# Causal top-8 attention in a ViT tower: keys from the centred stream, and a softmax shared out over DVE, ACT and Pool

## Chip, cores and metric

One core of a Trainium2 chip. The metric is the device time of one execution in microseconds (us). Engines: PE (TensorE, matmul), DVE (VectorE), ACT (ScalarE), Pool (GpSimd), SP (SyncE, which here only issues DMAs). All tiles of the passage are f32 unless said otherwise.

## The reference, cut to what matters

The kernel computes a tower of four layers on 16 images of 36 tokens with 64 features; after each attention and each feed-forward part stands `h = layernorm(h + part(h))`. The change lies in the attention of layer 2:

```python
Q = (x @ Wq.T).reshape(B, T, H, dh).transpose(0, 2, 1, 3)   # H = 4 heads, dh = 16, T = 36
K = (x @ Wk.T).reshape(B, T, H, dh).transpose(0, 2, 1, 3)
V = (x @ Wv.T).reshape(B, T, H, dh).transpose(0, 2, 1, 3)
scores = jnp.max(Q[:, :, :, None, :] + K[:, :, None, :, :], axis=-1)
scores = jnp.where(causal_mask[None, None], -jnp.inf, scores)
topk_vals, topk_idx = jax.lax.top_k(scores, k)              # k = 8
attn = jax.nn.softmax(topk_vals, axis=-1)
Vg = jnp.take_along_axis(V[:, :, None, :, :], topk_idx[..., None], axis=3)
ctx = jnp.einsum('bhtk,bhtkd->bhtd', attn, Vg)
```

The score is a maximum over a sum, not a dot product, and the softmax runs over the eight largest of the scores alone. `x` is the layer-normalised stream: centred per token, then multiplied by one over its standard deviation.

## The kernel before

576 tokens lie as [128, 288]: the two halves of the batch are stacked on partitions (64 features each), and a tile of 96 tokens per half is one of three (`NT` = 3, `TT` = 96). There are no loops over blocks of memory: each engine runs one long, hand-ordered list of instructions, and semaphores tie the lists together. An engine works its list strictly in order.

**Layernorm number k.** ACT squares the accumulated, already centred stream `psY` into `SQ` (semaphore `sq`). DVE copies it to `XC`, "centred" (`xc`). PE multiplies `SQ` with a mean matrix, which gives the variance with tokens on partitions (`variance(k)`, L376), ACT takes the root, DVE the reciprocal `RS`, [96 tokens, 6] (`rs`, L939). PE spreads `RS` over the features (`broadcast`, L383, called by `spread(k)`; `bc`), and DVE multiplies `XC` by it (`normalise(k, ...)`, L944), which gives `HP`, the normalised stream h (`hp`). `idle(n, bank)` (L369) issues n matmuls on a zero tile whose result nobody reads; they stand wherever PE would wait.

**Keys of layer 2.** For layernorm 4 PE runs `variance(4)`, `spread(4)`, waits for `hp`, and multiplies `HP` by `wk` (L589): the keys, with tokens on partitions, in PSUM (`k_done`). DVE splits them into three bf16 parts whose sum is the f32 value: `kp3[0]` a cast (L1149), the rest `k1f` a subtraction (L1151), `kp3[1]` a cast (L1152), `kp3[2]` a subtraction (L1154). Each adds one to `k_parts`. SP waits for each in turn and sends it to DRAM (L264); when all three have landed, one DMA brings them back, laid out by image, into `KB` (L267, `k_bcast`). Behind the keys PE makes queries (L592) and values (L598) out of `HP`; DVE, behind its key steps, splits the queries likewise (L1161 to L1168).

**Scores.** PE forms every sum q + k (L619, L621), and DVE takes the maximum over the 16 features of a head (L1177), 15 times, into `SC`, [128 queries, 5 x 4 rows, 40 keys], masked keys at -1e30.

**Softmax before.** On DVE: 20 `max` (MAX8, L1184) put the eight largest of each row, in order, into `top` (`topped`); 20 `match_replace` (L1188; each shows as a value load and a replacement) write to `REP` a copy of the row in which those eight are -3e30 (`replaced`). Then, each on all 20 x 40 elements of a partition: `REP` = (`SC` differs from `REP`), the selected ones (L1198); `SC` minus the row's maximum (L1199, `exp2_in`); ACT's exponential (L853, `exp2_out`); `PR` = the product with the selection (L1202); its row sum (L1203); reciprocal of 20 (L1204); `PR` times it (L1205, `prob2`). PE then transposes `PR` (L638), and the context follows. While it waits PE runs 7 dummy matmuls after the scores, 7 after `topped`, 7 after `replaced`, 4 after `exp2_in`, 7 after `exp2_out`.

Pool is in this time between two calls of `gates32` (L297), a small cast for the router, and has nothing to do.

## Time and profile before

| | us |
|---|---|
| median of 3 runs | 185.74 |
| lowest, highest | 184.01, 186.16 |
| the profiled execution: time | 185.84 |
| the profiled execution: span, first to last instruction | 184.1 |

| engine | busy us | share of the span |
|---|---|---|
| PE | 158.9 | 86% |
| DVE | 105.4 | 57% |
| ACT | 69.2 | 38% |
| Pool | 28.5 | 16% |

How to read it: a busy share is a mean over stages with different limits. PE's 86% holds 46.1 us of dummy matmuls, so it is no measure of a limit; what a stage is worth is read from the chain that ended last. In a row of a chain stand the start in us, the duration in us, and engine, tile and line. In a row of instruction groups stand the count, the busy time and the mean in ns of one, and behind the last bar the idle time before them.

### The profile page before, as it was taken

The numbers are of one execution on the slowest core, as the hardware profiler recorded it, in microseconds if no ns is written. First come the engines' busy times: TensorE is split into PE (matmuls) and PEld (weight loads), VectorE is DVE, ScalarE is ACT, GpSimd is POOL, SyncE is SP. The second block draws the span as 40 slices with busy tenths as digits, with TensorE's granted clock in tenths as the row PEclk, the third lists the DMA queues.
The fourth block names the chain that finished last, engine by engine and source line by source line (L and its number), as shares of the span: only waits on it lengthen the run. The fifth ranks groups of instructions, "written<-read, shape, count | busy, mean of one in ns | idle before, by whom it ended". The sixth has DMA issues, their size and how long they took to land.

```text
span 184.1 us, 2928 instructions
## 1 busy us (share of the span) xinstructions
PE 158.9 (86%) x1135; PEld 72.9 (40%) x1135; DVE 105.4 (57%) x324; ACT 69.2 (38%) x117; POOL 28.5 (16%) x79
## 2 busy tenths in 40 slices
PE   6999799899999988889978865699799997999950
PEld 2455366333333444334523121356333354573410
DVE  6224788454567374863756998716647422204884
ACT  3746906645460103634300000435723256563020
POOL 7300000187792000010000000000085000000000
PEclk9999999999999999999999999999999999996996
DMA  6999900000000000000220000000000000000001
GB/s 187 344 431 266 367 35 4 0 2 0 5 2 0 0 0 0 4 0 0 42 60 0 0 0 0 0 4 0 4 0 0 2 4 0 0 4 0 0 0 32
DMA packets 4916, 8.26 MB, mean 45 GB/s; under 512 B 2747, under 2 KB 2875, under 8 KB 4774
## 3 DMA queue, kind: packets, MB, share of 16 engines
q1 hardware_dynamic: 4902, 8.07, 13.5%
q8 instruction: 9, 0.15, 0.3%
q14 instruction: 5, 0.04, 0.1%
HBM read 7.70 MB, written 0.37 MB: 44 GB/s over the span
## 4 chain that ended last, share of the span: by engine, by line
PE 56%; DVE 27%; ACT 7%; DMA 5%; issue 3%; POOL 0%; DVEq 0%; ACTq 0%; POOLq 0%
PE ps L427 8%; PE ps L369 8%; PE ps L414 7%; DVE scores L1177 5%; PE ps L421 4%; PE ps L751 3%; PE ps L383 3%; PE ps L376 3%; DVE scores_rest L1188 2%; DMA k_scratch<-k_parts_tok 2%; DMA weights_sb<-weights 2%; PE ps L479 2%; PE ps L487 2%; DMA k_parts_img<-k_scratch 2%; DVE hidden_gated L998 2%
## 5 line engine op out<-in xcount | busy, mean ns | idle before, releaser
L369 PE MATMUL ps<-idle_operand 128*128 128x512 bf16 x170 | 46.1, 389 | 7.5 <-DVE scores_rest L1188 1.8
L998 DVE TENSOR_TENSOR hidden_gated<-hidden,ps 128x288 f32<-128x288 f32 x56 | 22.2, 450 | 14.6 <-PE ps L421 14.6
L787 ACT ACTIVATE hidden<-ps,weights_sb 128x576 f32<-128x576 f32 x28 | 20.2, 737 | 17.8 <-PE ps L414 15.4
L369 PEld LDWEIGHTS ps<-idle_operand 128*128 128x128 bf16 x170 | 14.5, 102 | 26.7 <-issue 5.3
L779 ACT ACT_TABLE_LOAD x16 | 20.5, 1283 | 0.3
L427 PE MATMUL ps<-hidden_gated,weights_sb 128*64 128x288 f32 x112 | 19.8, 432 | 0.9 <-DVE hidden_gated L998 0.8
L297 POOL CAST combine_parts_T<-combine_parts_T 48x288 f32<-48x288 bf16 x3 | 1.3, 418 | 105.6 <-DVE combine_parts_T L970 105.6
L767 ACT ACTIVATE squares<-ps 128x288 f32<-128x288 f32 x8 | 3.3, 410 | 33.6 <-PE ps L427 10.3
L414 PE MATMUL ps<-h,weights_sb 64*128 64x288 f32 x80 | 14.5, 449 | 1.0 <-ACT hidden L787 0.8
L936 DVE COPY centred<-ps 128x288 f32<-128x288 f32 x8 | 3.7, 456 | 18.0 <-ACT squares L767 18.0
L1177 DVE TENSOR_REDUCE scores<-ps 128x32 f32<-128x512 f32 (+1 forms) x15 | 8.8, 663 | 3.6 <-PE ps L621 3.6
L751 PE MATMUL ps<-weights_sb,hidden 128*128 128x512 f32 (+1 forms) x20 | 10.6, 689 | 0.0
L421 PE MATMUL ps<-combine_parts_T,selectors 128*128 128x288 bf16 x40 | 9.1, 292 | 0.8 <-DVE combine_parts_T L970 0.8
L414 PEld LDWEIGHTS ps<-h,weights_sb 64*128 64x128 f32 x80 | 6.3, 185 | 8.7 <-ACT hidden L787 4.7
L853 ACT ACTIVATE scores<-scores 128x800 f32<-128x800 f32 x1 | 0.9, 869 | 22.6 <-DVE scores L1199 22.6
L427 PEld LDWEIGHTS ps<-hidden_gated,weights_sb 128*64 128x64 f32 x112 | 5.5, 134 | 9.1 <-DVE hidden_gated L998 5.7
L414 PE MATMUL ps<-xn,weights_sb 64*128 64x288 f32 x32 | 5.6, 448 | 1.3 <-ACT hidden L787 1.3
L421 PEld LDWEIGHTS ps<-combine_parts_T,selectors 128*128 128x128 bf16 x40 | 3.0, 96 | 9.1 <-DVE hidden_gated L998 5.5
L751 PEld LDWEIGHTS ps<-weights_sb,hidden 128*128 128x128 f32 (+1 forms) x20 | 3.8, 199 | 6.3 <-issue 6.3
L376 PEld LDWEIGHTS ps<-consts_sb,squares 128*96 128x96 f32 x48 | 4.7, 164 | 3.9 <-ACT squares L767 3.9
L383 PE MATMUL ps<-consts_sb,rstd 96*64 96x96 f32 x108 | 6.2, 253 | 0.0
L619 PE MATMUL ps<-bconsts_sb,q_parts 128*128 128x512 bf16 (+1 forms) x15 | 5.7, 377 | 0.6 <-DMA k_parts_img<-k_scratch 0.6
(270 smaller groups left out, 225.4 us busy)
## 6 DMA issues: line engine op xcount, KB each, us to landing
patch_sb<-patches SPq DMA_DIRECT2D x6, 288.0 KB, 5.4
weights_sb<-weights SPq DMA_DIRECT2D x1, 1108.0 KB, 9.5
weights_sb<-weights SPq DMA_DIRECT2D x1, 717.0 KB, 15.5
weights_sb<-weights SPq DMA_DIRECT2D x1, 689.0 KB, 14.2
weights_sb<-weights SPq DMA_DIRECT2D x1, 640.0 KB, 7.3
weights_sb<-weights SPq DMA_DIRECT2D x1, 512.0 KB, 11.9
weights_sb<-weights SPq DMA_DIRECT2D x1, 394.0 KB, 12.9
weights_sb<-weights SPq DMA_DIRECT2D x1, 375.5 KB, 6.5
```

Of the source, the lines that this page charges most:

```text
L369: mm(PS[:, bank, :], idle_in[:, 0:P], idle_in[:, :], start=True, stop=True)
L376: last = mm(psVar[:, 2 * t:2 * t + 2], SQ[:, cols(t)], c("mean"), start=True, stop=True)
L383: last = mm(dst[rows(h), cols(t)], RS[:, at + 2 * t + h:at + 2 * t + h + 1].to_broadcast([TT, D]), c("ident", TT)[:, 0:TT], start=True, st ...
L414: last = mm(PS[:, z + h, 0:HALF], w1[rows(h), ch, :], src[rows(h), :], start=True, stop=True)
L421: mm(PS[:, G + h, 0:HALF], sel[:, g, h, :], CT3[:, :], start=True, stop=True)\
L427: last = mm(PS[rows(h), YB, 0:HALF], w2[:, ch, :], HG[:, ch % GRING, h, :], start=False, stop=(ch == chunks - 1), skip_group_check=True)
L619: mm(PS[:, n % 4, 0:keys * D].rearrange("p (s e) -> p s e", e=D), QA[:, j * P:(j + 1) * P], cb("id2").unsqueeze(1).to_broadcast([P, keys, ...
L751: last = mm(y3(q), tok3(q, ch), wd[:, ch, :], start=False, stop=(ch == 1), skip_group_check=True)
L779: act.activation(warm[:, tables[0]:tables[0] + 1], warm[:, 0:1], func)
L787: act.activation(HR[:, at % RING, :, :], two(ZA if ch % 2 == 0 else ZB), func, bias=w(f"b1_{n}")[:, ch:ch + 1]).then_inc(S["act_out"], 1)
L998: dve.tensor_tensor(HG[:, at % GRING, h, :], HR[:, at % RING, h, :], PS[:, G + h, 0:HALF], ALU.mult)\
L1177: dve.tensor_reduce(SC[:, j, :, 8 * g:8 * g + keys].rearrange("p h s -> p s h"), PS[:, n % 4, 0:keys * D].rearrange("p (s h d) -> p s h d" ...
```

## The change

Keys: PE multiplies the centred tile `XC`, not the normalised `HP`, by `wk`, between `variance(4)` and `spread(4)`; DVE multiplies the product by `RS`, which has tokens on partitions as the keys have, and then splits it. The multiplication that makes `HP` now stands on DVE behind the first key part. The dummy matmuls of `spread(4)` go to another PSUM bank, and the first group is 1, not 3.

Softmax: the sum over the eight selected exponentials is taken from `top` itself (tiles `TE`, 8 per row), since these are the selected values. Pool subtracts the maximum over all 40 keys (tile `SE`) in two parts, rows of 3 and of 2 of the five query groups, ACT takes the exponential of each part, and Pool multiplies each by the reciprocal of the sum. In the same time DVE runs its 20 replacement steps, with the sum and reciprocal between the eighth and the ninth. One last DVE operation, `scalar_tensor_tensor`, compares `REP` with -3e30 and multiplies by `SE`. `SE` and `TE` lie in the memory of the patches, which are long used.

```diff
--- before.py
+++ after.py
@@ -86,7 +86,7 @@
 logits exp_in exp_out onehot counted comb_split comb_turned comb_t ctf_ready gates z_done act_out gated y_done
 guard_read guarded
 lru_u lru_w
-k_done q_done v2_done q_hi q_parts k_parts k_bounce k_bcast v2_ready score_mm score_red exp2_in exp2_out
+k_done q_done v2_done q_hi q_parts k_parts k_bounce k_bcast v2_ready score_mm score_red top_in top_out top_sum sub2 exp2_out norm2
 prob2 prob2_t prob2_copied ctx2_done ctx2_ready
 x3_done x3_ready s3_done h3_t h3_copied exp3_in exp3_out p3_ready p3_t p3_copied
 h3_ready y3_done comb3_done bias3 bias3_split hres
@@ -174,6 +174,9 @@
         REP = sb("scores_rest", [P, QT, HEADS, SPAD])
         PR = sb("probs", [P, QT, HEADS, 64])
         top = sb("top8", [P, QT, HEADS, 8])
+        X1 = X[:, :, :].rearrange("p k t -> p (k t)")
+        SE = X1[:, 0:QT * HEADS * SPAD].rearrange("p (j h s) -> p j h s", j=QT, h=HEADS)
+        TE = X1[:, QT * HEADS * SPAD:QT * HEADS * (SPAD + 8)].rearrange("p (j h s) -> p j h s", j=QT, h=HEADS)
         d20 = [sb(f"row_stat{i}", [P, QT * HEADS]) for i in range(2)]
         PT = sb("probs_T", [P, 2, QT * P])
         VB = sb("v_blockdiag", [P, 2, IMAGES, 2 * DH])
@@ -349,6 +352,20 @@
             gates32(1)
             pool.wait_ge(S["w_r2"], 16)
             pool.tensor_scalar(WRG[:, :], w("Wr"), w("gam2"), None, ALU.mult).then_inc(S["wr_gam"], 1)
+            cut = ((0, 3), (3, QT))
+            pool.wait_ge(S["topped"], QT * HEADS)
+            for a, b in cut:
+                pool.tensor_tensor(SE[:, a:b, :, :].rearrange("p j h s -> p (j h) s"),
+                                   SC[:, a:b, :, :].rearrange("p j h s -> p (j h) s"),
+                                   top[:, a:b, :, 0].rearrange("p j h -> p (j h)").unsqueeze(2)
+                                   .to_broadcast([P, (b - a) * HEADS, SPAD]), ALU.subtract).then_inc(S["sub2"], 1)
+            pool.wait_ge(S["top_sum"], 1)
+            for n, (a, b) in enumerate(cut):
+                pool.wait_ge(S["exp2_out"], n + 1)
+                pool.tensor_tensor(SE[:, a:b, :, :].rearrange("p j h s -> p (j h) s"),
+                                   SE[:, a:b, :, :].rearrange("p j h s -> p (j h) s"),
+                                   d20[1][:, a * HEADS:b * HEADS].unsqueeze(2).to_broadcast([P, (b - a) * HEADS, SPAD]),
+                                   ALU.mult).then_inc(S["norm2"], 1)
             gates32(2)
             pool.wait_ge(S["bias3"], 16)
             link(pool.tensor_copy(BD3[0:1, :], BR[0:1, :]))
@@ -386,10 +403,11 @@
 
             def spread(k):
 
-                idle(1 if k in (1, 3) else 3, ZA)
+                bank = MB if k == 4 else ZA
+                idle(1 if k in (1, 3, 4) else 3, bank)
                 pe.wait_ge(S["rs"], k + 1)
                 broadcast(psBC, 0)
-                idle(2, ZA)
+                idle(2, bank)
 
             def residual(name, stop=False):
 
@@ -582,12 +600,13 @@
 
 
             variance(4)
+            pe.wait_ge(S["w_r2"], 16)
+            pe.wait_ge(S["xc"], 5)
+            for t in range(NT):
+                last = mm(PS[0:TT, ZA, t * P:(t + 1) * P], XC[:, cols(t)], w("wk"), start=True, stop=True)
+            last.then_inc(S["k_done"], 1)
             spread(4)
-            pe.wait_ge(S["w_r2"], 16)
             pe.wait_ge(S["hp"], 5)
-            for t in range(NT):
-                last = mm(PS[0:TT, ZA, t * P:(t + 1) * P], HP[:, cols(t)], w("wk"), start=True, stop=True)
-            last.then_inc(S["k_done"], 1)
             for h in range(2):
                 last = mm(PS[:, ZB + h, 0:HALF], w("wq2")[rows(h), :],
                           HP[rows(h), :].rearrange("p (b n) -> p n b", n=POS), start=True, stop=True)
@@ -625,12 +644,10 @@
             idle(7, MB)
             pe.wait_ge(S["topped"], QT * HEADS)
             idle(7, MB)
+            pe.wait_ge(S["top_sum"], 1)
+            idle(7, MB)
             pe.wait_ge(S["replaced"], QT * HEADS)
-            idle(7, MB)
-            pe.wait_ge(S["exp2_in"], 1)
             idle(4, MB)
-            pe.wait_ge(S["exp2_out"], 1)
-            idle(7, MB)
             pe.wait_ge(S["prob2"], 1)
             for pair in range(2):
                 z = flat2(ZA if pair == 0 else ZB, QT * P)
@@ -849,8 +866,11 @@
                     act.activation(VB[hp * 64:hp * 64 + POS, :, h * PER:(h + 1) * PER, hp * DH:(hp + 1) * DH],
                                    PS[hp * 64:hp * 64 + POS, G + h, 0:256].rearrange("p (b a d) -> p a b d", a=2, d=DH),
                                    ACT.Copy).then_inc(S["v2_ready"], 1)
-            act.wait_ge(S["exp2_in"], 1)
-            act.activation(SC[:, :, :, :], SC[:, :, :, :], ACT.Exp).then_inc(S["exp2_out"], 1)
+            act.wait_ge(S["top_in"], 1)
+            act.activation(TE[:, :, :, :], TE[:, :, :, :], ACT.Exp).then_inc(S["top_out"], 1)
+            for n, (a, b) in enumerate(((0, 3), (3, QT))):
+                act.wait_ge(S["sub2"], n + 1)
+                act.activation(SE[:, a:b, :, :], SE[:, a:b, :, :], ACT.Exp).then_inc(S["exp2_out"], 1)
             table(ACT.Sqrt)
             act.wait_ge(S["prob2_t"], 2)
             act.activation(PT[:, 1, :], flat2(ZB, QT * P), ACT.Copy).then_inc(S["prob2_copied"], 1)
@@ -1139,16 +1159,19 @@
 
 
             variance(4)
-            normalise(4, HP[:, :], "hp")
             dve.wait_ge(S["k_done"], 1)
+            dve.wait_ge(S["rs"], 5)
             psK = PS[0:TT, ZA, 0:NT * P].rearrange("p (t h e) -> p h t e", t=NT, h=2)
 
             def by_half(x):
                 return x.rearrange("p (h t e) -> p h t e", h=2, t=NT)
 
-            dve.tensor_copy(by_half(kp3[:, 0, :]), psK).then_inc(S["k_parts"], 1)
+            link(dve.tensor_tensor(by_half(k1f[:, :]), psK, RS[:, 0:2 * NT].rearrange("p (t h) -> p h t", h=2)
+                                   .unsqueeze(3).to_broadcast([TT, 2, NT, D]), ALU.mult))
+            dve.tensor_copy(kp3[:, 0, :], k1f[:, :]).then_inc(S["k_parts"], 1)
+            normalise(4, HP[:, :], "hp")
             dve.wait_ge(S["k_parts"], 1)
-            link(dve.tensor_tensor(by_half(k1f[:, :]), psK, by_half(kp3[:, 0, :]), ALU.subtract))
+            link(dve.tensor_tensor(k1f[:, :], k1f[:, :], kp3[:, 0, :], ALU.subtract))
             dve.tensor_copy(kp3[:, 1, :], k1f[:, :]).then_inc(S["k_parts"], 1)
             dve.wait_ge(S["k_parts"], 2)
             dve.tensor_tensor(kp3[:, 2, :], k1f[:, :], kp3[:, 1, :], ALU.subtract).then_inc(S["k_parts"], 1)
@@ -1183,26 +1206,24 @@
                 for h in range(HEADS):
                     dve.max(top[:, j, h, :], SC[:, j, h, :]).then_inc(S["topped"], 1)
             dve.wait_ge(S["topped"], QT * HEADS)
+            te20 = TE[:, :, :, :].rearrange("p j h s -> p (j h) s")
+            top20 = top[:, :, :, :].rearrange("p j h s -> p (j h) s")
+            dve.tensor_tensor(te20, top20, top20[:, :, 0:1].to_broadcast([P, QT * HEADS, 8]), ALU.subtract)\
+               .then_inc(S["top_in"], 1)
             for j in range(QT):
+                if j == 2:
+                    dve.wait_ge(S["top_out"], 1)
+                    link(dve.tensor_reduce(d20[0][:, :], te20, AX, ALU.add))
+                    dve.reciprocal(d20[1][:, :], d20[0][:, :]).then_inc(S["top_sum"], 1)
                 for h in range(HEADS):
                     dve.match_replace(REP[:, j, h, :], top[:, j, h, :], SC[:, j, h, :], 3 * NEG)\
                         .then_inc(S["replaced"], 1)
             dve.wait_ge(S["replaced"], QT * HEADS)
-            sc20 = SC[:, :, :, :].rearrange("p j h s -> p (j h) s")
-            rep20 = REP[:, :, :, :].rearrange("p j h s -> p (j h) s")
-            pr20 = PR[:, :, :, 0:SPAD].rearrange("p j h s -> p (j h) s")
-
-            def row20(x):
-                return x.unsqueeze(2).to_broadcast([P, QT * HEADS, SPAD])
-
-            link(dve.tensor_tensor(rep20, sc20, rep20, ALU.not_equal))
-            dve.tensor_tensor(sc20, sc20, row20(top[:, :, :, 0].rearrange("p j h -> p (j h)")), ALU.subtract)\
-               .then_inc(S["exp2_in"], 1)
-            dve.wait_ge(S["exp2_out"], 1)
-            link(dve.tensor_tensor(pr20, sc20, rep20, ALU.mult))
-            link(dve.tensor_reduce(d20[0][:, :], pr20, AX, ALU.add))
-            link(dve.reciprocal(d20[1][:, :], d20[0][:, :]))
-            dve.tensor_tensor(pr20, pr20, row20(d20[1][:, :]), ALU.mult).then_inc(S["prob2"], 1)
+            dve.wait_ge(S["norm2"], 2)
+            dve.scalar_tensor_tensor(PR[:, :, :, 0:SPAD].rearrange("p j h s -> p (j h) s"),
+                                     REP[:, :, :, :].rearrange("p j h s -> p (j h) s"), 3 * NEG,
+                                     SE[:, :, :, :].rearrange("p j h s -> p (j h) s"), ALU.is_equal, ALU.mult)\
+               .then_inc(S["prob2"], 1)
             dve.wait_ge(S["prob2_t"], 1)
             dve.tensor_copy(PT[:, 0, :], flat2(ZA, QT * P)).then_inc(S["prob2_copied"], 1)
```

## Rows read from the trace of the kernel before

**Rows 1.** The page, chain that ended last, share of the span by engine.
```profile
PE 56%; DVE 27%; ACT 7%; DMA 5%; issue 3%; POOL 0%; DVEq 0%; ACTq 0%; POOLq 0%
```

**Rows 2.** The same chain in order of time, key stretch: start us, us, what.
```profile
87.84 0.88 PE ps L589 x6
...
88.75 0.56 DVE k_parts_tok L1149
...
89.92 0.37 DVE k_parts_tok L1152
...
90.31 0.56 DVE k_parts_tok L1154
...
90.89 3.41 DMA k_scratch<-k_parts_tok
...
97.39 0.38 PE ps L619
```

**Rows 3.** Timeline of the key stretch: start us, us, instruction, [idle time before it].
```profile
85.19 0.46 DVE L936 COPY centred<-ps 128x288 f32<-128x288 f32 x1 [1.25 <-ACT squares L767]
85.21 0.67 PE L376 MATMUL ps<-consts_sb,squares 128*96 128x2 f32 x6
...
86.21 0.19 DVE L939 RECIPROCAL rstd<-std 96x6 f32<-96x6 f32 x1 [0.57 <-ACT std L772]
...
86.48 0.71 PE L383 MATMUL ps<-consts_sb,rstd 96*64 96x96 f32 x12
...
87.24 0.46 DVE L944 TENSOR_TENSOR h<-centred,ps 128x288 f32<-128x288 f32 x1 [0.84 <-PE ps L383]
...
90.79 0.81 DVE L1161 CAST q_parts<-ps 128x640 bf16<-128x640 f32 x1
```

**Rows 4.** The chain in order of time, softmax stretch.
```profile
106.85 2.14 DVE top L1184 x20
...
109.01 3.48 DVE scores_rest L1188 x21
...
112.52 1.00 DVE scores_rest L1198
...
114.57 0.88 ACT scores L853
...
116.50 1.00 DVE row_stat L1203
...
117.52 0.29 DVE row_stat L1204
...
118.88 1.20 PE ps L638 x9
```

**Rows 5.** Groups of instructions by shape, DVE and ACT, the nearest sizes.
```profile
L1060 DVE SCALAR_TENSOR_TENSOR weights_sb<-row_sums,weights_sb 128x1280 f32<-128x1280 f32 x1 | 1.5, 1484 | 0.0
L1244 DVE TENSOR_TENSOR gate_tmp<-logits_sb,gate_col 128x40 f32<-128x40 f32 x1 | 0.2, 201 | 0.0
...
L881 ACT ACTIVATE exp_sb<-s_sb 128x288 f32<-128x288 f32 x1 | 0.4, 442 | 0.9 <-DVE s_sb L1231 0.9
```

**Rows 6.** Groups of instructions by shape, Pool.
```profile
L322 POOL TENSOR_SCALAR decay<-decay,lru_par 128x576 f32<-128x576 f32 x1 | 1.7, 1724 | 0.0
...
L358 POOL TENSOR_TENSOR bias_rest<-bias_rows,bias_bf 1x512 f32<-1x512 f32 x1 | 1.1, 1147 | 0.1
...
L337 POOL TENSOR_TENSOR lru_sin_sb<-lru_sin_sb,lru_t 128x16 f32<-128x16 f32 x1 | 0.2, 218 | 0.1
```

**Rows 7.** The chain in order of time, a hand-over from DVE to Pool.
```profile
133.58 0.31 DVE combine_parts_T L970
...
133.94 0.43 POOL combine_parts_T L297
```

**Rows 8.** Busy time in two stretches: us, then each engine (count), PEclk, DMA.
```profile
107.00:119.00 12.00, 7.63 (x33) 2.72 (x32) 10.68 (x66) 2.35 (x3) 0.00 (x0) 1.00 0.00 0
164.00:172.00 8.00, 8.00 (x31) 3.94 (x31) 3.26 (x12) 1.79 (x4) 0.00 (x0) 0.79 0.01 2
```

## The prediction

> **What bounds the kernel now.** I read the chain of work that ended last first [rows 1]. It is mostly TensorE (PE), but not evenly. Up to about 84 us and from about 119 us it alternates quickly between engines in projections and expert networks that this change leaves alone. Between them lies the attention with top-8 selection, in three stretches. In the key stretch the chain in order of time goes from the normalised stream through six matmuls, four DVE steps and two DMA trips to the first score matmul at 97.39 us [rows 2]. In the score stretch, about 98 to 107 us, DVE reduces PSUM tiles; nothing there is edited. In the softmax stretch one row follows another, all on DVE but for one exponential on ACT, up to the transposes at 118.88 us [rows 4]. Over 107 to 119 us DVE is busy 10.68 us of 12.00 and GpSimd (Pool) 0.00; PE's 7.63 us are dummy matmuls that keep its clock at 1.00 [rows 8]. So whatever shortens the key chain or the softmax chain shortens the span one for one, as long as PE, which waits at the end of both, has nothing else to wait for.
>
> **Keys: what moves.** Before, the order is: centred copy, reciprocal (ends 86.21 + 0.19 = 86.40), broadcast of it by PE (to 87.19), DVE multiply that makes h (87.24 to 87.70), two dummies, six key matmuls (87.84 to 88.72), first DVE step at 88.75 [rows 2, 3]. After, the key matmuls read the centred tile, which is ready at 85.19 + 0.46 = 85.65. PE reaches them when its variance matmuls are done, 85.21 + 0.67 = 85.88. They end at 85.88 + 0.88 = 86.76. The per-token factor is ready at 86.40, so it is no wait. DVE then works, with 0.02 between its steps:
> - multiply by the factor out of PSUM, priced as the first cast of before, 0.56: 86.80 to 87.36
> - cast of the first part, now out of SBUF, as L1152, 0.37: 87.38 to 87.75. This releases the first DMA; before it was 89.31
> - the multiply that makes h, 0.46. Its broadcast follows one dummy (0.23, as 7.63 us make 33 matmuls [rows 8]) and takes 0.71: 86.76 + 0.23 + 0.71 = 87.70, so DVE goes from 87.77 to 88.23
> - subtract 0.56, cast 0.37, subtract 0.56, with gaps: third part at 89.78
>
> Before, the third part is at 90.31 + 0.56 = 90.87. It is the last of three and the second trip waits for all three, so the gain is 90.87 - 89.78 = 1.1 us. The spacing from second to third part stays the same, so I take the trip of the third part as it is, 3.41 us [rows 2]. What becomes later: h, by 0.53 us. Queued behind it are the query matmuls, but before they stood behind the key matmuls and the dummies, and now only behind the dummies; they start about 88.25 instead of 88.64, and DVE's query steps anyway begin only when the third key part is done (before at 90.79 [rows 3]), so they move 1.1 earlier with it. ScalarE waits there for values only. SP issues the same four DMAs in the same order. Bounds: nothing, if the DMA trips take back what is given to them; 1.6, if the first part is what counts (89.31 against 87.75). I take 1.1.
>
> **Softmax: what goes.** After the last MAX8 before: replacement steps 109.01 to 112.50, mask compare 1.00, subtraction of the maximum 1.00, exponential 0.88, masking multiply 1.00, row sum 1.00, reciprocal 0.29, normalising multiply 1.00; PE starts its transposes at 118.88 [rows 4] (of the five rows of 1.00 two stand there). That is 9.87 us from 109.01.
>
> **Softmax: what comes.** On DVE:
> - subtraction on the top-8 tile, 128x160. A 128x40 one is 0.20 [rows 5] and an 800-wide one 1.00 [rows 4], so 0.20 + 120/760 x 0.80 = 0.33: to 109.34
> - eight replacement steps of 3.48/20 = 0.174: 1.39, to 110.75. Beneath them ACT takes the exponential of 160 elements, under the 0.44 of 288 [rows 5], so its result (about 109.8) is no wait
> - sum of 160 elements 0.33 (the row sum of 800, L1203, costs 1.00 as the product-like steps do), reciprocal 0.29: 111.41, which releases Pool
> - twelve replacement steps, 2.09: 113.52
> - the one compare-and-multiply on 800 elements, whose kind takes 1.48 for 1280 [rows 5] and so about 1.00 for 800: 113.54 to 114.54
>
> Pool, which stood idle, gets four tensor operations, of 480, 320, 480 and 320 elements. The nearest rows of its kind are 0.22 for 16 elements and 1.15 for 512 [rows 6]: (1147 - 218)/496 = 1.87 ns an element over some 0.19. So 1.09 and 0.79. Subtractions: from 109.06 (a hand from DVE to Pool takes 0.05: 133.58 + 0.31 to 133.94 [rows 7]) to 110.15 and 110.94. The exponentials of the two parts take some 0.60 and 0.47, between 0.44 for 288 and 0.88 for 800: done at 110.8 and 111.5. Normalising starts when DVE's reciprocal is there, 111.46, and ends at 112.55 and 113.34. DVE's replacement ends at 113.52, so Pool is under cover by 0.2 us. PE can start its transposes 0.04 behind the tile, at 114.58 instead of 118.88: 4.3 us. ACT's reload of its table, behind the second exponential, still ends long before it is wanted. PE's queue gets one wait (for the reciprocal) with seven dummies, and loses two waits; four dummies of 0.23 behind the last replacement step end with the tile.
>
> Bounds of Pool's price: below 1.87 ns nothing more is won, since DVE is then last. Above, the dearest wide row is 1.72 for 576 elements of a scalar operation, (1724 - 190)/576 = 2.66 ns [rows 6]. Then the parts take 1.47 and 1.04, subtraction ends at 111.57, normalising at 114.08, the tile is at 115.1, and 3.7 us is saved instead of 4.3. I take the row of the same operation, 1.87.
>
> The row shows 1.87 ns an element for two inputs. The Trainium skill, GPSIMD Engine Reference, section 3.1, gives some 2.6 cycles an element for tensor_tensor, at the clock of 1.2 GHz that it states; as an estimate from that page 2.17 ns, Pool's normalising would end at about 113.6 and the sum would be 0.1 us worse. This case's row is cheaper and is used.
>
> **Sum.** 1.1 + 4.3 = 5.4 us. The profiled execution has a span of 184.1 and a time of 185.84, 1.7 outside the span. 185.84 - 5.4 = 180.4. The median of the runs shown, 185.74, is 0.1 lower, so I say 180.3, 2.9% less.
>
> **Rivals.**
> *Pool gets in first.* DVE's 160-wide subtraction and Pool's first subtraction are both let go by the last MAX8. If they can't run together and Pool starts first, DVE waits 1.09 and all that follows on it is as much later: 181.4. Against it: DVE goes on 0.02 after its own result (108.99 to 109.01 [rows 4]), Pool after 0.05 [rows 7].
>
> This rival follows a rule of the Trainium skill (SBUF — State Buffer, "Who interferes with whom"): a DVE instruction with two SBUF inputs and a GpSimd instruction that reads SBUF share a read port, and the one that starts second waits for the whole of the other. With DVE first it costs Pool 0.3 us while it has slack, and by the same page the replacement steps, of one input each, don't contend. No row of before has such a pair side by side.
>
> *Full serialisation.* If every replacement step stands still while Pool works, DVE's 4.5 us and Pool's four operations, 4 x 0.19 + 1600 x 1.87 = 3.75 us, add up: tile at 109.01 + 4.5 + 3.75 + 1.0 = 118.3, only 0.6 won; with the keys 1.7: 184.1, no change. For: no row shows Pool reading beside these steps. Against: they have one input tensor each.
>
> *Keys gain nothing.* The DMA trips give the 1.1 back: 181.4.
>
> *A clock dip.* PE's granted clock has a mean of 0.79 over 164 to 172 us [rows 8]: of its two levels it stood at the lower, 1.2 GHz, for 0.21 x 8 x 2 = 3.4 us, and lost half of them, 1.7 us. PE was busy 8.00 of those 8.00 us by its records, so it fell without a long wait. The new order shifts everything behind 86 us and shortens the dummy stretches; another dip costs up to 1.7: 182.0. The one that is there may vanish: 178.6. For the forecast: the stretch of 12 us with 7.63 us of dummies stayed at 1.00, and the new one is denser: behind the last MAX8 it has 18 dummies in 5.5 us, the old one 25 in 9.9.
>
> *Slower.* Pool's price per element over 800-wide, three-dimensional, broadcast operands is unseen. It decides alone if it is high: the four operations then run one after the other, and the saving of both parts, 5.4 us, is eaten when the tile comes at 114.54 + 5.4 = 119.9, that is when 1600 p = 119.9 - 1.0 (compare-and-multiply) - 109.06 - 4 x 0.19 - 0.1 (gaps) = 9.0 us, p = 5.6 ns, three times the row of its kind and twice the dearest. At p = 8 ns the time is 189.6, over 2% slower.
>
> **Numbers.** Two per cent is about what a measurement of this kernel can tell from no change: under 182.0 (0.98 of 185.7) counts as faster, over 189.5 as slower. Forecast, with Pool's price up to its upper row, 180.3 to 180.9: 0.55. Pool first 0.08, keys nothing 0.05, a further dip 0.15, the dip gone 0.03, serialisation 0.09, Pool over 5.6 ns 0.05. The range from the vanished dip to the further dip with Pool's upper price (182.0 + 0.6) is 178.6 to 182.6 and holds about 0.83. The likeliest case's own range is 179.8 to 181.0. Faster: 0.54 + 0.08 + 0.05 + 0.03 + a third of the dip, which ends on the bound = 0.75; slower: 0.04, from Pool at over 5.6 ns and dips on top; same: the rest, 0.21.
>
> **What the profile after will show.** Key matmuls right behind the variance matmuls, first key part near 87.8 and third near 89.8, first score matmul near 96.3. From the last MAX8 to the transposes 5.5 us. Pool's 480-wide operations near 1.1 us; 20 replacement steps still 0.17 each (if they stretch, it is serialisation); DVE's 160-wide subtraction 0.33 (if 1.4, Pool was first). I am wrong if DVE stands waiting for Pool before the last compare-and-multiply for more than 0.6 us, or if the clock falls between 105 and 130 us.

## The result, and the profile after

The changed kernel takes 178.38 us (177.98 to 178.78, 4 runs) against 185.81 for the kernel before in the same comparison: ratio 0.962, 95% interval 0.956 to 0.968. That is 3.8% faster; forecast were 180.3 and 2.9%, and the time lies 0.2 us below the low end of the range, 178.6. Six more executions gave 177.97 to 178.75. Ratios here and below leave out executions that lie over 1.5% above the fastest of the same kernel.

The profiled execution has a span of 176.9 (before 184.1). Its chain in order of time (start us, us, what), which answers to [rows 2, 4]:

```profile
85.78 0.79 PE ps L606 x6
...
86.60 0.56 DVE k_rest L1169
...
87.19 0.36 DVE k_parts_tok L1171
87.54 0.38 DVE h L964
87.92 0.47 DVE k_rest L1174
...
88.42 0.37 DVE k_parts_tok L1175
...
88.81 0.56 DVE k_parts_tok L1177
...
89.39 3.73 DMA k_scratch<-k_parts_tok
...
93.14 3.20 DMA k_parts_img<-k_scratch
...
96.47 0.38 PE ps L638
...
105.94 2.14 DVE top L1207 x20
...
108.10 0.32 DVE patch_sb L1211
108.42 1.36 DVE scores_rest L1219 x9
109.78 0.24 DVE row_stat L1216
...
110.27 1.86 DVE scores_rest L1219 x11
...
113.39 1.31 PE ps L655 x10
```

The reader sees the key matmuls (L606) ahead of h (L964), the third part ready at 89.37 instead of 90.87, and both DMA trips longer than before, 3.73 and 3.20 against 3.41 and 2.94. Behind the last MAX8 the chain has only DVE steps, 5.3 us instead of 9.9. Pool lies beside it in the timeline, and the last operation starts on DVE's own step:

```profile
108.15 1.84 POOL L358 TENSOR_TENSOR patch_sb<-scores,top 128x480 f32<-128x480 f32 x2 [28.06 <-DVE top L1207]
...
110.40 1.67 POOL L365 TENSOR_TENSOR patch_sb<-patch_sb,row_stat 128x480 f32<-128x480 f32 x2 [0.41 <-DVE row_stat L1217]
...
112.33 0.99 DVE L1223 SCALAR_TENSOR_TENSOR probs<-scores_rest,patch_sb 128x800 f32<-128x800 f32 x1
```

Pool's second group starts as soon as DVE's reciprocal is there (0.41 idle) and ends at 112.07, 0.26 ahead of 112.33.

The end of the kernel, by stretch (us; busy time and count of PE, PEld, DVE, ACT, Pool; granted clock). This is the stretch of [rows 8] that lies as far behind the transposes:

```profile
158.50:166.50 8.00, 7.96 (x33) 4.33 (x34) 4.61 (x15) 1.80 (x4) 0.00 (x0) 1.00 0.01 2
```

The clock is 1.00 where it was 0.79. The ledger of the two spans (the differences of the starts named):

| stretch | before | after | won |
|---|---|---|---|
| up to the squares of layernorm 4 | 84.75 | 84.65 | 0.10 |
| from there to the first score matmul | 12.64 | 11.82 | 0.82 |
| scores and MAX8 | 11.60 | 11.61 | 0.0 |
| last MAX8 to first transpose | 9.89 | 5.30 | 4.6 |
| transposes to the end | 65.22 | 63.52 | 1.7 |

The squares of layernorm 4 start at 84.75 before and 84.65 after. So 5.4 of the 7.2 us lie where the change is, and 1.7 where nothing was edited.

### The profile page after: what moved, and what is told of

Read it like the earlier page. It is cut to its first block, busy times and chain, and to the rows that moved or that the text cites. A ratio compares the mean times of both kernels' runs of the same rounds, so it can differ in the third digit from the quotient of the medians.

```text
span 176.9 us, 2902 instructions
## 1 busy us (share of the span) xinstructions
PE 153.0 (86%) x1110; PEld 71.9 (41%) x1126; DVE 102.1 (58%) x323; ACT 69.7 (39%) x119; POOL 32.1 (18%) x83
## 4 chain that ended last, share of the span: by engine, by line
PE 56%; DVE 26%; ACT 7%; DMA 6%; issue 3%; POOL 0%; DVEq 0%; ACTq 0%; POOLq 0%
PE ps L445 9%; PE ps L386 8%; PE ps L432 7%; DVE scores L1200 5%; PE ps L439 4%; PE ps L393 3%; PE ps L400 3%; PE ps L768 2%; DMA k_scratch<-k_parts_tok 2%; DVE scores_rest L1219 2%; DMA weights_sb<-weights 2%; DMA k_parts_img<-k_scratch 2%; PE ps L505 2%; PE ps L497 2%; DVE hidden_gated L1018 2%
## 5 line engine op out<-in xcount | busy, mean ns | idle before, releaser
L386 PE MATMUL ps<-idle_operand 128*128 128x512 bf16 x145 | 40.9, 390 | 7.4 <-issue 1.9
L386 PEld LDWEIGHTS ps<-idle_operand 128*128 128x128 bf16 x161 | 13.7, 102 | 23.5 <-issue 5.3
L784 ACT ACTIVATE squares<-ps 128x288 f32<-128x288 f32 x8 | 3.3, 410 | 33.6 <-PE ps L445 10.3
L768 PE MATMUL ps<-weights_sb,hidden 128*128 128x512 f32 (+1 forms) x20 | 9.0, 600 | 0.0
L358 POOL TENSOR_TENSOR patch_sb<-scores,top 128x480 f32<-128x480 f32 (+1 forms) x2 | 1.8, 940 | 28.1 <-DVE top L1207 28.1
## 6 DMA issues: line engine op xcount, KB each, us to landing
weights_sb<-weights SPq DMA_DIRECT2D x1, 512.0 KB, 11.8
```

Of the source, the lines that this page charges most:

```text
L386: mm(PS[:, bank, :], idle_in[:, 0:P], idle_in[:, :], start=True, stop=True)
L768: last = mm(y3(q), tok3(q, ch), wd[:, ch, :], start=False, stop=(ch == 1), skip_group_check=True)
```

## The experiments

**The two halves alone.** `keys_only` is the kernel before with the key hunks of the diff, `soft_only` with the softmax hunks.

> The kernel before with the key part of the change alone. Theory (the ledger of the two profiles: keys 0.8 us, softmax 4.6 us, and 1.7 us from a clock dip at the end that is gone): the third key part is ready about 1.4 us sooner and the first score matmul 0.8 to 1.4 us; time 184.7 to 185.0 if PE's clock still dips near 167 us, 183.0 to 183.3 if it doesn't. Rival (the keys are worth all of the gain that the softmax row by row does not explain, 2.6 us): 183.2 with the dip in place.

183.08 us (182.49 to 184.40) against 185.30: 0.989 (0.984 to 0.994).

> The kernel before with the softmax part of the change alone. Theory: 5.3 us from the last MAX8 to the transposes instead of 9.9; time 185.8 - 4.6 = 181.2 with the dip, 179.5 without. Rival (the softmax gives back part of its gain where it stands alone): over 182.

179.41 us (179.05 to 180.21): 0.969 (0.965 to 0.972). From the last MAX8 to the transposes it has 5.3 us, as the full change. The halves come to 2.2 and 5.9 us against the median of before, 8.1 together, more than the 7.4 us of the whole change. In the profiled executions each of these differences holds the 1.7 us of the end once; how much of it is in the medians is not known, since some of the other executions may have paid it. By stretch the halves add up: in `keys_only` the first score matmul comes 11.6 us behind the squares instead of 12.6, which is 1.0, and the softmax gives 4.6. In the profiles of both, the end from the transposes on takes 63.52 us. In `keys_only` the first DMA trip is again longer than before (3.82 against 3.41), the second is not (2.90 against 2.94):

```profile
88.82 3.82 DMA k_scratch<-k_parts_tok
...
92.66 2.90 DMA k_parts_img<-k_scratch
```

**Where the 1.7 us come from.** The kernel before was profiled once more.

> The kernel before, unchanged, once more. Theory: the dip of PE's clock near 167 us is in most of its executions, 185.8 with it and about 184.1 without, as one of four runs so far showed 184.01. Rival: the dip is always there and 184.01 was a shorter DMA trip.

It took 183.65 us, and its end took 63.54, as in the kernel after. In the same form as above, two stretches of it:

```profile
164.00:172.00 8.00, 8.00 (x32) 4.07 (x31) 5.12 (x18) 1.72 (x3) 0.00 (x0) 1.00 0.00 0
104.00:112.00 8.00, 5.45 (x17) 1.78 (x16) 7.90 (x66) 0.00 (x0) 0.00 (x0) 0.79 0.00 0
```

A spell of the lower clock of the same length, 0.21 x 8 x 2 = 3.4 us, is there too, but at 104 to 112 us, where DVE is busy 7.90 of 8.00 and PE only waits beside it with dummies. There it costs nothing: from the last MAX8 to the transposes this execution took 9.9 us, as long as the one on which the prediction rests. So the spell is not tied to a place; its price is. The 40 timed executions of the kernel before that ran beside the experiments fall in two groups: 22 from 185.06 up (median 185.6), all with a mean clock of 0.981 or less, and 18 from 182.9 to 184.5 (median 184.1), of which 15 have 0.987 or more and 3 have 0.980 to 0.982, as `before_again` had with its spell that was not paid for; these three were not profiled. The profiled execution on which the prediction rests, 185.84, is one of the first group. The expected rival, that the dip is always there near 167 us, falls; 184.01 needs no shorter DMA trip.

A mean clock says only in part whether a spell was paid for, since it holds the last microseconds of the kernel too. The kernel after, mean 0.991, in the same form at its end:

```profile
175.00:176.90 1.90, 0.00 (x0) 0.00 (x0) 0.00 (x0) 0.00 (x0) 0.00 (x0) 0.50 0.16 35
```

The lower clock here costs nothing, as PE has no work left. Only the clock of the stretch in which PE works on the chain tells.

> The kernel after, unchanged. Theory (a 3.4 us spell of PE's lower clock falls somewhere in many executions of any of these kernels, and costs up to 1.7 us only where PE sets the end): its times split in two groups about 1.3 us apart by their mean clock, as those of the kernel before do (184.3 to 184.5 at a mean clock of 0.996, 185.3 to 185.7 at 0.98), with some executions at 179.5 to 180. Rival (the change has done away with the spell): all executions near 178.4, none above 179.

Six executions, 177.97 to 178.75, median 178.58: 0.966 (0.961 to 0.971). Half have a mean clock of 0.982 or 0.983, so the spell is not done away with (the rival falls), yet by their times none paid for it. In the profiled one the clock is at the lower level (0.50) over 107 to 109 us, in the softmax stretch, and the end takes 63.5 us. The prediction had named a clock that falls between 105 and 130 us as a sign of being wrong; it fell there, and cost nothing, since DVE set the end of that stretch. The expected two groups of times were not seen either. Ten executions of the kernel after, none of which paid, stand against 22 of 40 of before. Whether that is the later stages' new place in time or luck is open: a spell that is paid for came back in other versions with the same end (below).

**Pool beside DVE.** Pool's work put on DVE, in the same two parts, the subtractions ahead of the replacement steps and the multiplications behind them (these are moved in the same way):

```diff
-            pool.wait_ge(S["topped"], QT * HEADS)
-            for a, b in cut:
-                pool.tensor_tensor(SE[:, a:b, :, :].rearrange("p j h s -> p (j h) s"),
...
+            for a, b in ((0, 3), (3, QT)):
+                dve.tensor_tensor(SE[:, a:b, :, :].rearrange("p j h s -> p (j h) s"),
...
```

> The kernel after, but the subtraction and the normalising of all 800 elements run on DVE, in the same two parts, and Pool stands idle. Theory (Pool's work is wholly under DVE's replacement steps): DVE gets 4 operations of 0.66 and 0.49 us, 2.3 us, and the time is 178.4 + 2.3 = 180.7. Rival (Pool's reads hold DVE's steps up, so that taking them away gives something back): under 180.2.

181.37 us (180.64 to 182.11): 0.980 (0.976 to 0.984). Groups by shape on DVE (mean ns):

```profile
L1200 DVE TENSOR_TENSOR patch_sb<-scores,top 128x480 f32<-128x480 f32 x1 | 0.7, 652 | 0.0
L1200 DVE TENSOR_TENSOR patch_sb<-scores,top 128x320 f32<-128x320 f32 x1 | 0.5, 484 | 0.0
```

The softmax stretch took 7.37 us, 2.1 more than with Pool, and the two executions with a mean clock of 0.987 took 180.64 and 181.07, close to the 180.7 expected; the other two, at 0.98, took 181.68 and 182.11, so that the median is 0.7 above it. The two instructions of a replacement step lasted as long without Pool (187 and 81 ns) as with it in the kernel after (184 and 79). Moving the work to Pool is worth 2.1 us. That leaves 2.5 of the 4.6 for the rest of the edit: fewer wide steps, a sum over 160 elements instead of 800, and an exponential that no longer stands alone; these were not tried one by one.

The order turned round:

```diff
-            dve.tensor_tensor(te20, top20, top20[:, :, 0:1].to_broadcast([P, QT * HEADS, 8]), ALU.subtract)\
-               .then_inc(S["top_in"], 1)
...
                 for h in range(HEADS):
+                    if j == 0 and h == 2:
+                        dve.tensor_tensor(te20, top20, top20[:, :, 0:1].to_broadcast([P, QT * HEADS, 8]),
+                                          ALU.subtract).then_inc(S["top_in"], 1)
```

> The kernel after with DVE's 160-wide subtraction behind the second replacement step, so that Pool's first subtraction is under way when DVE comes to it. Theory of the shared read port: the subtraction can't run until Pool's operation is over, so it ends about 0.8 us later or more than its place in the list says, and the transposes come 0.8 to 1.5 us later. Rival (they run side by side): it takes 0.32 and nothing else moves; the transposes come 5.3 us behind the last MAX8 as before.

Timeline of Pool and DVE:

```profile
107.11 1.79 POOL L358 TENSOR_TENSOR patch_sb<-scores,top 128x480 f32<-128x480 f32 x2 [27.84 <-DVE top L1207]
...
107.40 0.90 DVE L1218 TENSOR_TENSOR patch_sb<-top 128x160 f32<-128x160 f32 x1
```

DVE's subtraction, 0.32 us in the kernel after, lasted 0.90 when Pool's first one was under way, and ended at 108.30, some 0.2 behind the end of Pool's first part (107.11 + about 1.0). The stretch took 5.89 instead of 5.31: the whole 0.58 was paid, less than the 0.8 to 1.5 expected. This was one execution, and its time of 178.29 does not show the 0.58, because its squares of layernorm 4 came 0.8 us earlier (83.83 against 84.65). The two replacement steps beside the same Pool operation lasted 0.18 as ever. So the prediction's rival "Pool gets in first" is real in kind, and the order of the list decides it. With DVE first, Pool's first part took 1.15; the same subtraction done again with DVE out of the way took 1.02 (`pool_double`, below). The cost is then 0.13 us of slack.

This is the rule of the Trainium skill, SBUF — State Buffer, "Who interferes with whom": two SBUF inputs on DVE and a reading GpSimd operation share one port, and whoever starts second waits. The trace agrees for DVE as the second (0.58 us), and for the replacement steps with one input, which did not wait. With Pool as the second it agrees in kind; Pool's record was longer by 0.13 us, while the two records lie side by side for 0.27.

Pool's subtractions done twice:

```diff
             pool.wait_ge(S["topped"], QT * HEADS)
+            for a, b in cut:
+                link(pool.tensor_tensor(SE[:, a:b, :, :].rearrange("p j h s -> p (j h) s"),
...
             for a, b in cut:
```

> The kernel after, in which Pool does each subtraction twice, 1.84 us more. Theory (Pool has 0.4 us of slack ahead of the reciprocal and 0.26 us at the end): the last compare-and-multiply starts 1.84 - 0.41 - 0.26 = 1.2 us later, so 5.3 + 1.2 = 6.5 us from the last MAX8 to the transposes; the replacement steps stay at 0.17 each. Rival (Pool slows DVE's steps): they stretch, and it is over 7 us.

Its timeline, Pool and the last DVE operation:

```profile
109.47 1.71 POOL L363 TENSOR_TENSOR patch_sb<-scores,top 128x480 f32<-128x480 f32 x2
...
111.26 1.68 POOL L370 TENSOR_TENSOR patch_sb<-patch_sb,row_stat 128x480 f32<-128x480 f32 x2
...
113.04 0.99 DVE L1228 SCALAR_TENSOR_TENSOR probs<-scores_rest,patch_sb 128x800 f32<-128x800 f32 x1 [1.47 <-POOL patch_sb L370]
```

The stretch took 6.75 us against 6.5 expected, and DVE now waits 1.47 us for Pool. It had been 5.31, so 1.96 us more on Pool (107.43 to 109.39 for the extra pair) cost 1.44. The replacement steps did not stretch. Pool's slack in the kernel after is some 0.5 us. (This too was one execution. Its 181.0 us hold a paid spell: its clock was 0.79 over 159 to 167 us, and its end took 65.1.)

**The DMA trips.** h put behind all three key parts, and 6 dummies instead of 10 behind the query parts:

```diff
             dve.tensor_copy(kp3[:, 0, :], k1f[:, :]).then_inc(S["k_parts"], 1)
-            normalise(4, HP[:, :], "hp")
...
             dve.tensor_tensor(kp3[:, 2, :], k1f[:, :], kp3[:, 1, :], ALU.subtract).then_inc(S["k_parts"], 1)
+            normalise(4, HP[:, :], "hp")
...
             pe.wait_ge(S["q_parts"], 3)
-            idle(10, MB)
+            idle(6, MB)
```

> The kernel after with the multiply that makes h behind all three key parts on DVE, and 6 dummy matmuls instead of 10 behind the query parts. Theory (the chain goes through the third key part and the two DMA trips, and queries have slack): third part 0.38 us sooner, query parts 1.4 us later but still 1.5 us before the keys are back, first score matmul 0.4 us sooner: 178.0. Rival (the trips take back what they are given, as 0.6 of the 1.4 us in the kernel after): no change, 178.4. Second rival: queries become the last to arrive, 179.

179.68 us (177.74 to 183.47): 0.972 (0.965 to 0.978). The first score matmul came 11.2 us behind the squares of layernorm 4 instead of 11.6 to 11.8: as far as the theory said, but for another reason. The three transfers of the first trip, issue to landing:

```profile
DMA to landing us min/median/max: 1.9/1.9/1.9
```

In the kernel after the same line has a maximum of 3.7, and before 3.4: it is the third transfer, the one the chain waits for. Here it took 1.9. The keys were back early, and the chain went through h, the query parts (ready 94.02) and the 6 dummies, as the second rival had it. What the long trips have in common stands in the DMA view of the kernel after, 89.3 to 93.2 us:

```profile
q1 hardware_dynamic: 1184, 0.15, 25.8%
q8 instruction: 1, 0.02, 2.3%
```

One packet of 16 KB on an instruction queue: it started at 90.5 and took 1.41 us, amid the small packets of the key parts. The same view for 91.0 to 91.8 and for 91.8 to 92.3 us shows what became of them:

```profile
DMA packets 0, 0.00 MB, mean 0 GB/s; under 512 B 0, under 2 KB 0, under 8 KB 0
...
DMA packets 19, 0.01 MB, mean 21 GB/s; under 512 B 18, under 2 KB 18, under 8 KB 18
```

All but 18 small packets had started by 90.9; the last 18 came when the packet of 16 KB was over, and the transfer landed at 93.1. In `h_last` the fetch came at 91.5, when the first trip was over; there the second trip took 3.6 us instead of 2.9 to 3.2. The next kernel moves only this fetch. It puts 80 small matmuls into a wait of PE that lies 20 us earlier:

```diff
             idle(9, MB)
+            for _ in range(80):
+                mm(PS[0:32, MB, 0:16], idle_in[:, 0:32], idle_in[:, 0:16], start=True, stop=True)
```

> The kernel after with 80 small extra matmuls (32 columns of weights, 16 columns moved) in an earlier wait of PE, at about 68 us, where PE is idle for 1.45 us; nothing else. They lengthen PE's instruction stream, so that its instruction fetch of 16 KB, which in the profiles of before and after falls inside the first DMA trip of the keys, comes some 160 instructions earlier. Theory (the fetch holds up one of the DMA engines that carry the third key part, and the trip takes 3.3 to 3.8 us with it and 1.9 without, as in the kernel with h behind the key parts): the trip takes 1.9, keys are back 1.8 us sooner, and the first score matmul is then held by the query parts and the 10 dummies behind them, 1.2 us sooner: 177.2. Rival (the short trip in that kernel had another reason): the trip stays at 3.6 to 3.8 and the time at 178.5.

The fetch came at 84.1, so it is PE's own instruction stream that is loaded there. The DMA view of 89.4 to 91.5 us shows no instruction packet, and:

```profile
q1 hardware_dynamic: 1184, 0.15, 47.0%
...
k_scratch<-k_parts_tok SPq DMA_DIRECT2D x1, 72.0 KB, 1.9
```

The third transfer took 1.9 us with everything around it as in the kernel after, so the fetch was the cause: without it the trip is 1.8 us shorter. It need not be the direct cause of all 1.8. In the kernel after a second instruction packet, 8 KB on queue 14, came at 92.1, still inside the delayed trip; in `pad` it came at 92.2, when the trip had landed (91.4). In `before`, `before_again` and `soft_only` it came behind the landing, and the trip took 3.4, 3.3 and 3.3; in `after`, `after_again` and `keys_only` it came inside, and the trip took 3.7, 3.7 and 3.8. So the 0.3 to 0.5 us by which the trip was longer after than before may be this packet's; no run moved it alone. The first score matmul came 10.5 us behind the squares, 1.1 to 1.3 sooner. And yet the time was 179.27 us (177.38 to 179.85): 0.969 (0.963 to 0.976). Four of six executions have a mean clock of 0.97. The profiled one is of these and shows two spells, one paid and one free:

```profile
158.00:166.00 8.00, 8.00 (x27) 3.73 (x26) 3.73 (x13) 1.72 (x3) 0.00 (x0) 0.79 0.00 0
103.00:111.00 8.00, 6.05 (x21) 2.41 (x21) 7.90 (x67) 2.90 (x5) 3.52 (x4) 0.79 0.00 0
```

Its end took 65.13 us, 1.6 more than 63.52. The two executions with 0.99 took 177.38 and 177.60, 0.9 to 1.1 us under the medians of the kernel after (178.38 and 178.58); 177.2 was expected. Why so many executions of this version paid is open.

The last hunk of `h_last` alone:

```diff
             pe.wait_ge(S["q_parts"], 3)
-            idle(10, MB)
+            idle(6, MB)
```

> The kernel after with 6 dummy matmuls instead of 10 behind the query parts; nothing else. Theory (dummies missing while PE waits for the keys bring PE's lower clock, which made the kernel with h behind the key parts scatter from 177.7 to 183.5): median 179 to 180, mean granted clock 0.97 to 0.98 in most executions. Rival (there the wait for h, 1.57 us, did it, and these dummies don't matter): 178.5 at 0.982 to 0.991.

177.95 us (177.53 to 178.70), mean clocks 0.983 to 0.990. The first score matmul came 11.4 us behind the squares, against 11.6 to 11.8 in the kernel after. The theory fell: in four executions the lack of these four dummies cost no clock. What made `h_last` scatter (mean clocks 0.946 to 0.996) is open; the wait of PE for h was not tried alone.

Values later in PE's list, in the kernel after:

```diff
-            for b8 in range(PER):
...
-            last.then_inc(S["v2_done"], 1)
-            residual("ident")
...
-            idle(8, ZA + 1)
+            idle(15, ZA + 1)
             pe.wait_ge(S["wr_bet"], 1)
             pe.wait_ge(S["q_parts"], 3)
-            idle(10, MB)
+            for b8 in range(PER):
...
+            last.then_inc(S["v2_done"], 1)
+            residual("ident")
+            idle(3, MB)
```

> The kernel after with the value matmuls and the residual behind the query parts in PE's list, 15 dummies ahead of that wait instead of 8, and 3 behind them instead of 10. Theory (the fetch falls behind the first trip, since PE issues fewer instructions ahead of it): the trip takes 1.9, and PE is free for the scores at 92.9 + 0.8 + 0.75 + 0.7 = 95.2 instead of 96.5: 177.2, if the clock stays up. Rival (fetch and second trip meet): 0.5 to 1.5 us of the gain are given back there.

178.11 us (177.48 to 180.37): 0.964 (0.957 to 0.972). The fetch came at 94.2, the third transfer took 1.9, and the first score matmul came 10.3 us behind the squares, so neither trip met it. The executions range from 177.48 at a mean clock of 0.996 to 180.37, whose profile has a spell twice as long in the end (0.57 over 158.5 to 166.5 us). That end took 66.75 us, 3.2 more than 63.52: twice the length, twice the price.

Last, the two edits together, the 80 small matmuls of `pad` and the 6 dummies of `few_dummies`:

> The kernel after with both: the 80 small matmuls at about 68 us, and 6 dummies instead of 10 behind the query parts. Theory (with the short trip the keys are back at about 94.3, and what held the first score matmul in the padded kernel were the dummies): it starts 0.8 us sooner than there, 9.6 to 9.8 us behind the squares of layernorm 4 instead of 10.5; executions without a paid clock spell near 176.7, with one near 178.3; the median depends on how many have one. Rival (keys come back later than that): the start moves by less than 0.4 us, best executions near 177.3.

177.60 us (176.61 to 179.83): 0.961 (0.955 to 0.967). Its chain:

```profile
89.20 1.88 DMA k_scratch<-k_parts_tok
...
91.09 3.21 DMA k_parts_img<-k_scratch
...
94.44 0.38 PE ps L640
```

The score matmul waits for nothing but the keys, 10.0 us behind the squares: 0.5 us sooner than in `pad`, between the two expectations (0.8 and under 0.4), since the second trip took 3.2. Its three executions with a mean clock of 0.99 or more took 176.6 to 177.1; two at 0.97 took 178.1 and 178.2, and one 179.8. The median is 0.8 to 1.0 us under that of the kernel after, the best execution 1.4; the two were not timed in one comparison, and the intervals of their ratios overlap, so that it beats the kernel after is likely, not shown.

The key stretch of the profiled executions side by side (us; start of the squares of layernorm 4, start of the first score matmul, the time between them, third transfer from issue to landing, start of the fetch of 16 KB nearest to it):

| kernel | squares | score matmul | apart | third transfer | fetch |
|---|---|---|---|---|---|
| `before` | 84.75 | 97.39 | 12.6 | 3.4 | 91.7 |
| `before_again` | 84.31 | 96.86 | 12.6 | 3.3 | 90.6 |
| `after` | 84.65 | 96.47 | 11.8 | 3.7 | 90.5 |
| `after_again` | 84.85 | 96.48 | 11.6 | 3.7 | 90.9 |
| `few_dummies` | 83.82 | 95.26 | 11.4 | 3.6 | 89.5 |
| `h_last` | 84.28 | 95.46 | 11.2 | 1.9 | 91.5 |
| `pad` | 84.76 | 95.27 | 10.5 | 1.9 | 84.1 |
| `v2_late` | 84.63 | 94.93 | 10.3 | 1.9 | 94.2 |
| `pad6` | 84.45 | 94.44 | 10.0 | 1.9 | 83.6 |

## Why the prediction was right, and by how much each step was off

The direction, the mechanism and the sum of the two stretches came as forecast. The time came out 0.2 us under the range, and by a case, the clock dip gone, that had been given a chance of 0.03.

**The chain.** Both shortened stretches were on it, and PE had nothing else to wait for. Right.

**Keys, 1.1 us.** The gain of the third part was sized 1.1 and was 1.5, or 1.4 from the same start. DVE's first step came at 86.60, not 86.80, and h at 87.47, not 87.77: I added groups of PE matmuls end to end, but records of neighbouring groups overlap by 0.1 to 0.2 us, and the next group issues that much sooner; DVE's own steps overlap too, by up to 0.1. The step "I take the trip of the third part as it is" held in kind and was off in size: 3.73 + 3.20 instead of 3.41 + 2.94 took 0.6 back. Net 0.8 instead of 1.1. Unseen in it was PE's instruction fetch: the price of the trip was 1.9 plus a delay of 1.4 to 1.9 us, present before and after alike. The named bound of 1.6 was too low for what the stretch can give; with two further edits, the fetch out of the way and fewer dummies, it gave 2.6 (10.0 against 12.6).

**Softmax, 4.3 us.** Measured 4.6. The small steps were right: 0.32 for the 160-wide subtraction (0.33 forecast), 0.99 for the last operation (1.00), twenty replacement steps unchanged. The 0.3 more is again overlap: where a step of another kind follows without a wait, its record starts up to 0.1 us before the other's end. Pool's price, 1.87 ns an element from rows with other shapes, gave 1.09 and 0.79; measured were 0.99 to 1.02 and 0.73 to 0.74 free of DVE, and 1.15 for the wider one with DVE in the way. The slack at the end, 0.2 forecast, was 0.26.

**The rivals.** Serialisation: no, the replacement steps kept their 0.17 us. Pool first: did not happen, but does when the list lets it. Keys nothing: in part; the trips gave back 0.6 of the 1.4 us. Pool at 5.6 ns an element: no.

**The clock.** This is the term that was mis-sized. The sum of 5.4 us was right to 0.1 for the edited stretches, and that by luck: the keys gave 0.3 less and the softmax 0.3 more than forecast. What it was taken from was not: the profiled execution of before had paid 1.7 us for a spell of the lower clock in its end, and I gave its vanishing a chance of 0.03. The times shown beforehand, 184.01 next to 185.74 and 186.16, were a sign of it. Unpaid executions of before have a median of 184.1; 184.1 - 5.4 = 178.7, and measured were 178.4 and, in the second comparison, 178.6. "The dip gone", 178.6, was the case that came, though not as it was worded: the lower clock still comes, at places where it costs nothing.

## What to carry to other kernels

Before a sum is taken from one profiled execution, look for stretches with a granted clock under 1.00 on PE's part of the chain and ask whether the median pays for them too: here 1.7 of the 7.2 us came and went with them. The mean clock of an execution is no substitute for the look, since it also counts stretches in which PE is off the chain or done. A transfer on the chain that takes longer than others of its size should be checked for an instruction fetch beside it; it moves with the number of PE instructions ahead, which an edit far away can change. When Pool is given tensor operations beside DVE, put DVE's operations with two inputs in SBUF first in the list, or where Pool does not read, and price Pool's slack on both sides of its waits.

## What the runs showed of the hardware that was not expected

- A 16 KB instruction fetch for PE of 0.9 to 1.6 us, nine in an execution, lengthened a transfer of 72 KB that ran beside it from 1.9 to between 3.3 and 3.8 us; shown by moving the fetch (1.9 in `pad`). In the kernel after all but 18 of the small packets had started within its first 0.4 us; for the next 1.0 none started, and the last 18 came when it was over.
- The spell of the lower clock lasts 3.4 us in most profiles, wherever it falls; it came in stretches where PE's records are 100% busy (end of before) and 68% (softmax stretch) alike, and cost 1.6 to 1.7 us or nothing (one of twice the length 3.2). What decides in which executions and where it falls is open.
- A DVE operation of 0.32 us with two SBUF inputs took 0.90 when Pool was reading; one-input steps beside it did not change.
